# A fused attention and expert kernel: attention unrolled, order of a slot changed, banks and weights laid out anew

## What is computed

```python
x = x + _L0_xattn_ref(_layernorm(x, axis=-1), ctx_2048, Wq, bq, Wk, bk, Wv, bv, Wo, bo)
x = x + _L0_ffn_ref(_layernorm(x, axis=-1), ...)

def _L0_xattn_ref(x, c, Wq, bq, Wk, bk, Wv, bv, Wo, bo):
    q = jnp.einsum('oc,bct->bot', Wq, x) + bq[None, :, None]
    k = jnp.einsum('oc,bct->bot', Wk, c) + bk[None, :, None]
    v = jnp.einsum('oc,bct->bot', Wv, c) + bv[None, :, None]
    ...
    scores = jnp.einsum('bhkt,bhks->bhts', q, k) * SCALE
    p = jax.nn.softmax(scores, axis=-1)
    out = jnp.einsum('bhts,bhks->bhkt', p, v)
    ...
    return jnp.einsum('oc,bct->bot', Wo, out) + bo[None, :, None]
```

## Time and profile before

| | us |
|---|---|
| median of 3 runs | 1015.87 |
| lowest, highest | 1015.41, 1021.47 |
| span of the profiled execution | 1009.2 |
| TensorE busy in it | 892.0 (88%) |
| VectorE busy | 529.8 (52%) |
| ScalarE busy | 416.4 (41%) |
| first score matmul of slot 0 | 84.5 |
| first score matmul of slot 13 | 531.7 |
| last slot's end, start of the expert part | about 614 |

### The profile page before, as it was taken

How to read it: one execution, slowest core, us unless ns; L and a number is a source line. 1 busy time by engine, 2 the same in 40 slices (tenths; PEclk the granted TensorE clock), 3 DMA queues, 4 the chain that set the end, 5 groups by cost and what they waited for, 6 DMA issues and landing times. The chain is left out here.

```text
span 1009.2 us, 13687 instructions
## 1 busy us (share of the span) xinstructions
PE 892.0 (88%) x3632; PEld 374.6 (37%) x3633; DVE 529.8 (52%) x1049; ACT 416.4 (41%) x750; POOL 182.4 (18%) x192
## 2 busy tenths in 40 slices
PE   7479988998998989989988898999499999999982
PEld 3223333333323333333331224654144444444431
DVE  5487865686667858667866826442011111111156
ACT  0113655665664656556655884220022222222200
POOL 4351112012211211120220000017300000000075
PEclk7787999999998999999998997989699999999996
DMA  7436444355345445444552112918422222222178
GB/s 250 122 97 145 117 131 129 91 149 148 86 121 150 124 96 149 128 131 95 142 161 60 36 26 67 311 75 290 166 79 97 85 92 95 84 93 94 62 228 272
DMA packets 71194, 127.93 MB, mean 127 GB/s; under 512 B 15104, under 2 KB 37632, under 8 KB 68032
## 3 DMA queue, kind: packets, MB, share of 16 engines
q1 hardware_dynamic: 55600, 84.98, 31.3%
q0 software_dynamic: 9392, 31.20, 9.1%
q10 hardware_dynamic: 6160, 11.27, 3.0%
HBM read 76.70 MB, written 50.72 MB: 126 GB/s over the span
## 5 line engine op out<-in xcount | busy, mean ns | idle before, releaser
L515 ACT ACTIVATE probs<-st_ps 128x512 f32<-128x512 f32 x492 | 279.9, 599 | 217.8 <-PE st_ps L617 214.9
L709 DVE TENSOR_REDUCE negmax<-smax_ps 128x1 f32<-128x512 f32 x512 | 324.1, 680 | 73.3 <-PE smax_ps L592 73.0
L592 PE MATMUL smax_ps<-k_stack,q_stack 96*128 96x512 bf16 x512 | 204.9, 403 | 45.9 <-DVE negmax L709 33.4
L617 PE MATMUL st_ps<-q_stack,k_stack 99*128 99x512 bf16 x492 | 192.9, 395 | 13.5 <-ACT probs L515 11.1
L1181 PE MATMUL big_ps<-w_gu,pv_raw 128*128 x312 | 142.9, 601 | 1.4 <-DMA stretch<-in_L_ffn_w_down 1.4
L630 PE MATMUL pv_ps<-probs,v_t 128*32 128x512 f32 x1024 | 137.2, 608 | 2.1 <-ACT probs L515 1.1
L592 PEld LDWEIGHTS smax_ps<-k_stack,q_stack 96*128 96x128 bf16 x512 | 51.2, 100 | 200.8 <-DVE negmax L709 133.5
L435 POOL TENSOR_TENSOR rest<-qk,parts 128x512 f32<-128x512 f32 x32 | 36.9, 1152 | 358.3 <-DVE parts L699 358.3
L1338 DVE TENSOR_TENSOR zeros<-attn,big_ps 128x256 f32<-128x256 f32 x39 | 16.4, 421 | 139.9 <-ACT attn L1040 139.9
L617 PEld LDWEIGHTS st_ps<-q_stack,k_stack 99*128 99x128 bf16 x492 | 48.7, 99 | 108.8 <-ACT probs L515 76.6
L1181 PEld LDWEIGHTS big_ps<-w_gu,pv_raw 128*128 128x128 f32 x312 | 57.1, 193 | 59.2 <-issue 59.1
(11 more groups left out here) (132 smaller groups left out, 770.7 us busy)
## 6 DMA issues: line engine op xcount, KB each, us to landing
parts_dram<-parts SPq DMA_DIRECT2D x32, 384.0 KB, 4.1
blocks_in<-zeros POOLq DMA_DIRECT2D x39, 256.0 KB, 3.8
attn<-blocks_in SPq DMA_DIRECT2D x39, 256.0 KB, 2.6
k_stack<-parts_dram SPq DMA_DIRECT2D x16, 384.0 KB
q_stack<-parts_dram SPq DMA_DIRECT2D x16, 384.0 KB
blocks_out<-rms_bc ACTq DMA_DIRECT2D x20, 256.0 KB, 2.0
blocks_out<-recip ACTq DMA_DIRECT2D x19, 256.0 KB, 2.0
x_sb<-in_x SPq DMA_DIRECT2D x8, 512.0 KB, 7.3
```

Source lines behind the costliest of these rows:

```text
L515: nc.scalar.activation(probs[:, k0 % 2, u % GH, :], score_bank(s0, u)[0], ACT.Exp, scale=SCALE).then_inc(exp_done, 1)
L592: nc.tensor.matmul(smax_ps[:, u % MAXBUF, :], q_stack[n0s][0:SROWS, u // TT, tt * P:(tt + 1) * P], k_stack[n0s][0:SROWS, u // TT, :], star ...
L617: nc.tensor.matmul(bank, k_stack[n0s][0:SROWS + PARTS, GH * g + j, st * P:(st + 1) * P], q_stack[n0s][0:SROWS + PARTS, GH * g + j, :], sta ...
L709: nc.vector.tensor_reduce(negmax[:, n0 % 2, u:u + 1], smax_ps[:, u % MAXBUF, :], AX_X, ALU.max, negate=True).then_inc(max_done, 1)
```

## The change

- `slots`, the loops and their register arithmetic are gone; all 16 slots are written out.
- Weights and biases come laid out from the host: three DMAs, no transposes, no copies. The context loads are issued first on POOL.
- SP's list in a slot: `denominators` is cut into five steps, `write_parts` and `load_stacks` into single ones, and they alternate; `rows` is the last step.
- `invert` moves from unit 8 to 14, `divide` from unit 17 to 23, the output projection from the even slot 2b+2 to the odd slot 2b+3 (`out_batch`).
- Three banks for maxima and three for scores in all slots. ScalarE's copy of pv waits for the writes of two halves before, not of the last.

```diff
-MAXBUF = 4
+MAXBUF = 3
+STBUF = 3
...
+        def out_batch(s):
+
+            return (s - 3) // 2 if s % 2 == 1 and s >= 3 else None
+
+        def smax_bank(i):
+            return smax_ps[:, i % MAXBUF, :]
+
+        def score_bank(i):
+            return st_ps[:, i % STBUF, :]
...
-                for i, w in enumerate((wk, wq, wv, wo)):
-                    sp.dma_start(w_raw[:, i, :, :], w.rearrange("(o p) c -> p o c", p=P)).then_inc(w_loaded, 16)
...
+                sp.dma_start(w_t[:, :, :, :], wqkv_t).then_inc(w_loaded, 16)
+                sp.dma_start(bias[:, :, :], bias_cols).then_inc(b_loaded, 16)
+                sp.dma_start(w_o[:, :, :], wo_t).then_inc(w_loaded, 16)
...
+                def load_stack(n, i):
+                    dst = (k_stack, q_stack)[i][n % NBUF]
+                    if n >= NBUF:
+                        sp.wait_ge(st_ready, UNITS * (n - NBUF + 1))
+                    sp.wait_ge(parts_written[i], 16 * (n + 1))
+                    by_channel = parts_dram[n % NBUF, i].rearrange("s (i h) t -> s i (h t)", h=HH)
+                    for part in range(PARTS):
+                        count = PARTS - part
+                        g = PRODUCTS - count * (count + 1) // 2
+                        src = (by_channel[part:part + 1].broadcast_to([count, KCH, HH * T]) if i == 1
+                               else by_channel[0:count].rearrange("s i f -> (s i) f"))
+                        sp.dma_start(dst[KCH * g:KCH * (g + count), :, :].rearrange("p h t -> p (h t)"), src
+                                     ).then_inc(stack_loaded[n % NBUF], 16)
...
-                def slot(s0, it, loop):
-                    if loop or s0 > 0:
-                        denominators(sp, s0 - 1, it)
-                    if loop or s0 + 3 < HALVES:
-                        write_parts(s0 + 3, it)
-                    if loop or s0 + 1 < HALVES:
-                        rows(s0 + 1, it)
-                    if loop or s0 + 3 < HALVES:
-                        load_stacks(s0 + 3, it)
-
-                slots(sp, slot)
+                for s in range(HALVES):
+                    proj = s + 3 < HALVES
+                    if s > 0:
+                        numerators_out(sp, s - 1)
+                        den_in(sp, s - 1)
+                        num_in(sp, s - 1)
+                    if proj:
+                        write_part(s + 3, 0)
+                        load_stack(s + 3, 0)
+                    if s > 0:
+                        rec_out(sp, s - 1)
+                    if proj:
+                        write_part(s + 3, 1)
+                    if s > 0:
+                        rec_in(sp, s - 1)
+                    if proj:
+                        load_stack(s + 3, 1)
+                    if s + 1 < HALVES:
+                        rows(s + 1)
```

More of the change, by code:

```diff
@@ L196, in sync_wait @@
                     sp.wait_ge(sem, reg)
[L198 to L216, removed]
         X1_START = CT + 1
@@ L267, in project_out @@
+            if kt == 0 and (b > 0 or o > 0):
+                pe.wait_ge(x1_ready, X1_START + 2 * b + o)
+            mm = nc.tensor.matmul(bank, w_o[:, kt, o * P:(o + 1) * P], attn[:, b % 2, kt, :],
                                   start=(kt == 0), stop=(kt == CT - 1))
@@ L393, in _ @@
+                for n in range(2):
+                    for i in range(2):
+                        write_part(n, i)
+                        load_stack(n, i)
+                for i in range(2):
+                    write_part(2, i)
+                rows(0)
+                for i in range(2):
+                    load_stack(2, i)
                 sp.dma_start(rms_bc[:, :], rms_w.rearrange("(o d) -> o d", o=1).broadcast_to([P, D])).then_inc(shared_loaded, 16)
@@ L604, in scores, with turn_max @@
-                def scores(s0, u, it):
-                    bank, wait_exp = score_bank(s0, u)
+                    nc.tensor.matmul(smax_bank(i), q_stack[buf][0:SROWS, u // TT, tt * P:(tt + 1) * P],
+                                     k_stack[buf][0:SROWS, u // TT, :], start=True, stop=True).then_inc(s_ready, 1)
+                def turn_max(n):
+                    pe.wait_ge(vt_copied, min(n + 3, HALVES))
+                    if n > 0:
+                        pe.wait_ge(nm_copied, n)
+                    if n > 0 and out_batch(n - 2) is not None:
+                        pe.wait_ge(x1_ready, X1_START + CT * (out_batch(n - 2) + 1))
+                    pe.wait_ge(max_done, UNITS * (n + 1))
+                    nc.tensor.transpose(proj_ps[0:UNITS, 0:P], negmax[:, n % 2, :], ident[:, :]).then_inc(nm_turned, 1)
@@ L678, in tail @@
-                def tail(s0, it, loop):
-                    pv(STEPS * s0 - 1, it)
-                slots(pe, slot, tail, [pe.alloc_register(f"round{i}") for i in range(2)])
+                            project_v(s + 3, u - 12)
+                        if u == 18 and s + 1 < HALVES:
+                            turn_max(s + 1)
+                        if out_batch(s) is not None and u in OUT_UNITS:
+                            project_out(pe, out_batch(s), OUT_UNITS.index(u) // CT, OUT_UNITS.index(u) % CT, proj_ps[:, :])
@@ L801, in slot @@
                             row_scale(dve, 0, EARLY, 2, (u // 6,))
-                slots(dve, slot)
         attn_ctx.close()
```

564 lines of the change are left out of this document (250 added, 314 removed).

## The result

Before and after were timed in turn on one chip, four runs each: 1018.58 us (1015.41 to 1021.47) and 1128.41 us (1123.35 to 1134.94). The ratio of after to before is 1.112, 95% interval 1.107 to 1.118. The kernel became about 110 us slower. The forecast was 1131 us, with a range of 1055 to 1160. Some executions of this program run in a slower state at a lower granted clock; ratios and intervals here are of the other runs alone, medians of all.

What follows compares the result with a forecast made beforehand. The q load's tail on few DMA engines delayed denominators, stalling TensorE; after the change it would hold the rows. Prologue gain, longer slots and -2 us summed to +115 on span 1009.2, plus 6.7: 1131 us, range 1055 to 1160.

Steps and rivals of the forecast that it cites:

- The mechanism: Each slot border: the rows' write lands only when the q load drains, and TensorE waits; slots of 43.4 us, chance 0.77.
- One sign of being right: Before each of slots 1 to 13 TensorE waits 10 to 14 us, ended by the load of q_stack from rows_dram.
- slot 0 starts: Prologue: 3.3 us gained, bounds 0 and 5.2, so the first slot starts at 81.2 instead of 84.5.
- k stack issued in the slot: After a slot's first score matmul: k low parts at 13.6 us, their write about 4.1 us, k load issued at 17.8.
- q stack issued in the slot: Within a slot: the q parts' write, issued at 20.1 us, passes the k load and lands at 23.6; q load issued then.
- The 17.6 us taken from another stretch: Prologue's time from q stack 0's issue to the first maximum pass, taken as the q load's drain time in every slot.
- Slots 13 to 15: Last slots: reciprocal stall goes, one output projection moves from 14 to 15, last slot has fewer score banks; -2 us in all.
- From the span to the time: Whole kernel: the median of 1015.87 lies 6.7 us above the profiled span, so span 1124 becomes 1131 us.
- Rival B: Slots: the q load alone drains sooner, in 12.7 us; slots of 38.5 us, about 1067 us; chance 0.13.
- Rival C: Slots: the rows' write is not held up, TensorE sets the slot; about 49 us faster, 967 us; chance 0.04.
- Rival D: Division at unit 23: waits for reciprocals held up by the k load; another 3 us a slot, 1167 us; chance 0.06.
- Nothing where another wait sets the slot: Score and maximum banks: at most some 2 us a slot either way, and nothing where another wait sets the slot.

## Why the prediction was right, step by step

**The mechanism.** Confirmed: the rows' small write is held until the q load is drained, and TensorE waits for it at each slot border. Shown from both sides, by taking the order out of the changed kernel (-120 us) and putting it into the old one (+134 us against the old kernel's median beside it). In the first 2 us of each of slots 1 to 13 the clock was 0.50, as forecast. One sign of being right did not come: TensorE should have waited 10 to 14 us before each of slots 1 to 13, and it waited 4.8 to 16.9, 8.5 on average. The slot is as long as forecast, but TensorE comes to its end later: in slots 0 to 12 it is busy 32.9 us a slot where it was 31.9, and idles another 1.9 us elsewhere, part of it at the division (2.61 us in slot 3). Slots 1 to 12 spread from 39.7 to 46.2 us, wider than the 42 to 45 named.

**The terms on the span.** Predicted +115 us, measured +121.5 (1009.2 to 1130.7):

| step | predicted | measured |
|---|---|---|
| slot 0 starts | 81.2 | 81.6 |
| k stack issued in the slot | 17.8 | about 15.8 |
| q stack issued in the slot | 23.6 | about 24.2 |
| from there to the issue of the rows' reload | 17.6 + 0.2 | about 16.7 |
| from there to the next slot | 2.0 | 2.1 |
| a slot, mean of 1 to 12 | 43.4 | 43.0 |
| slot 0 | 46.8 | 46.5 |
| slot 13 starts | 649 | 644.3 |
| slots 13 to the last score matmul | 79.1 - 2 | 81.5 |
| behind it | 398.4 | 404.9 |

The slot is right as a sum; its terms are off by up to 2 us in both directions. k's stack went out sooner, q's a little later, the drain was some 1.1 shorter.

**The 17.6 us taken from another stretch held.** The risk of that step was that no row showed the rows' write behind a q load; 32 partitions were held like 4 and 128, 16.7 us on average and 14.6 to 19.9 from slot to slot.

**Slots 13 to 15.** I took -2. Slots 13 and 14 did gain, 4.9 us together (57.9 where before has 62.8), but the last slot has three score banks where it had six: 23.5 us instead of 16.3. The step named this edit and priced it too low. That slot now also holds the last output projection of the slots, but it is a small part of it: with the projection moved back and two score banks the slot took 23.1 us.

**From the span to the time.** I added 6.7 us because the median of before lay that far above its profiled span. This step was wrong. In all runs on record the time lies only 1.7 to 2.3 us above the run's own span; before's profiled span of 1009.2 would then belong to an execution of about 1011 us, faster than all four timed ones, and the other 4.7 us come from that one short execution and say nothing of the kernel after. The kernel after's profiled run took 1132.4 us, 1.7 above its span, and its median of 1128.41 lies below both. Both kernels' runs fall into two groups, 1015.4 to 1015.9 and 1021.3 to 1021.5 before, 1123.4 to 1124.4 and 1132.4 to 1134.9 after. The last stretch of the trace, from the first of the 32 closing gathers (`stretch<-blocks_out`) on, shows a difference of that size: 49.7 us in before's profiled run, 55.3 in after's, with this wait only in the latter:

```profile
1110.62 3.75 PE L1010 MATMUL tr_ps<-sh_dn,pv_raw 128*128 128x512 f32 x4 [5.36 <-DVE x_sb L1140]
```

The other kernels' profiled runs have either some 50 or some 55 us there, whatever was changed in attention. That this wait makes the two groups within one kernel is argued from the size, not shown. The span was forecast 6.5 us too low and this step was 9.0 too high, so the forecast of 1131 came within 2.6 us of the median by luck, closer than its parts.

**Rival B** asked how much of the 17.6 us is tail and how much volume. In the changed kernel about 6.5 are tail (16.7 against 10.2 with an even load, although its issue takes some 1 us longer); its forecast for this kernel was wrong, its question was not. **Rival C** (rows not held) would need another queue at least, and even there the write took 6.5 us. **Rival D** was right in its mechanism and wrong in its place: the division waits for reciprocals 25.3 us in all in the changed kernel, mostly hidden, since the slot ends with the rows' landing in any case, and it becomes the bound once that wait is gone (41.9 us with the rows first, 55.3 with the even load). I gave it only as an addition; it also limits what the change could have brought with a better order.

**"Nothing where another wait sets the slot"** for banks fits the changed kernel, but no run varies the banks in it. For the late output projection I had no term of its own at all, only the move from slot 14 to 15; with the old order its place costs some 2% (ratios of 1.017 and 0.999).

## What to carry over

A small DMA that an engine waits for belongs ahead of a large load in its queue, above all ahead of a load whose shape puts most rows on few DMA engines; in SP's list of a slot the place of two 24 KB transfers was worth 120 us. Before reordering around such a load, make the load even: the same bytes in six DMAs of 16 rows gave 5.5% in the old kernel with no other change. And before moving work into another slot, look at what already stands there: with the output projection beside the normalization VectorE's stall was 8.2 us and TensorE's 4.8, apart from it 5.9 and 2.5.

## What was not expected of the hardware

- An evenly spread load of 768 KB also holds a small write behind it, 9 to 12 us from the load's first issue; splitting removes the tail, not the volume.
- A write on POOL's queue, issued 0.5 us after SP's q load, landed within 6.0 us where in SP's own queue it took 14 (median 14.2 in the changed kernel, 6.5 on POOL's).
- The last slot took 16.3 us with six score banks and 23.1 to 24.7 with two or three, with or without the output projection in it.
- The same stretch behind the slots took 38.5 us at a mean granted clock of 0.87 and 44.5 at 0.73, in kernels whose work there is the same; what decides between the two is open.
